# Mixture-of-experts stage: the order of gathers and scatters, identity products at the end, and four idle products on TensorE

## The reference, cut to what matters

```
logits = flat_x @ gate_w.T
scores = softmax(logits).T                     # 16 experts x 2048 tokens
topk_weight, topk_idx = top_k(scores, C)       # C = 256 tokens for each expert
xg = flat_x[topk_idx]                          # gather
g = einsum('ecd,eid->eci', xg, Wg)
u = einsum('ecd,eid->eci', xg, Wu)
h = gelu(g) * u
eo = einsum('eci,edi->ecd', h, Wd) * topk_weight[..., None]
flat_out = zeros.at[topk_idx].add(eo)          # scatter, summed
out = flat_out + shared(x)
x = x + 0.5 * out
```

## Time and profile before

| what | value |
|---|---|
| median of 3 runs | 1263.83 us (1261.38 to 1265.91) |
| the profiled execution's own time | 1263.55 us |
| its span in the trace | 1261.7 us |
| PE busy | 1143.5 us, 91% |
| DVE busy | 865.9 us, 69% |
| ACT busy | 706.6 us, 56% |
| POOL busy | 523.4 us, 41% |

### The profile page before, as it was taken

How to read it: one execution, slowest core, us unless ns; L and a number is a source line. 1 busy time by engine, 2 the same in 40 slices (tenths; PEclk the granted TensorE clock), 3 DMA queues, 4 the chain that set the end, 5 groups by cost and what they waited for, 6 DMA issues and landing times. The chain is left out here.

```text
span 1261.7 us, 19699 instructions
## 1 busy us (share of the span) xinstructions
PE 1143.5 (91%) x6491; PEld 571.9 (45%) x6491; DVE 865.9 (69%) x1903; ACT 706.6 (56%) x887; POOL 523.4 (41%) x548
## 2 busy tenths in 40 slices
PE   4799999999999998869977599999999999778995
PEld 2444444444444484459963122222222223447994
DVE  6466566576666555864436999999999994585442
ACT  3677777777777625212215267767777677421221
POOL 0066666656656600337863013213311321035884
PEclk9899999999999997879998599999999999797998
DMA  4000011001001100516754421232132120322665
GB/s 123 1 7 25 18 26 38 17 24 40 17 24 34 36 18 31 174 29 190 179 107 82 84 64 42 61 51 59 43 64 53 37 51 1 136 70 86 177 160 117
DMA packets 58444, 81.91 MB, mean 65 GB/s; under 512 B 18520, under 2 KB 40412, under 8 KB 57500
## 3 DMA queue, kind: packets, MB, share of 16 engines
q1 hardware_dynamic: 46808, 71.87, 21.4%
q0 software_dynamic: 10944, 8.92, 4.7%
q10 hardware_dynamic: 616, 0.14, 0.1%
HBM read 55.34 MB, written 11.67 MB: 53 GB/s over the span
## 5 line engine op out<-in xcount | busy, mean ns | idle before, releaser
L1771 ACT ACTIVATE at_PR<-psum 128x1024 f32<-128x1024 f32 x256 | 248.0, 1021 | 121.8 <-PE psum L2000 121.6
L1839 DVE TENSOR_REDUCE at_MX<-psum 128x1 f32<-128x512 f32 x468 | 301.0, 685 | 10.5 <-PE psum L1982 6.1
L1708 POOL TENSOR_TENSOR at_PR<-at_PR,at_FAC 128x512 f32<-128x512 f32 x64 | 81.2, 1268 | 293.0 <-ACT at_PR L1771 293.0
L486 ACT ACTIVATE PR<-psum 128x1024 f32<-128x1024 f32 x144 | 140.9, 1026 | 82.2 <-PE psum L770 76.6
L770 PE MATMUL psum<-Q,K 64*128 64x512 f32 (+3 forms) x768 | 143.5, 502 | 1.2 <-ACT PR L486 1.2
L491 ACT ACTIVATE PR<-PR 128x1024 f32<-128x1024 f32 x144 | 144.6, 1062 | 0.0
L782 PE MATMUL psum<-PR,V 128*64 128x512 f32 (+3 forms) x768 | 139.7, 495 | 0.1
L2000 PE MATMUL psum<-at_QS,at_KS 122*128 122x512 bf16 x512 | 136.0, 387 | 2.2 <-DVE at_MX L1835 1.6
L2018 PE MATMUL psum<-at_PR,at_VG 128*32 128x512 f32 x1024 | 136.6, 606 | 0.0
L463 POOL TENSOR_SCALAR_AFFINE_SELECT PR<-PR 128x256 f32<-128x256 f32 (+1 forms) x112 | 57.7, 529 | 167.8 <-ACT PR L491 167.7
L1982 PE MATMUL psum<-at_KM,at_QM 64*128 64x512 bf16 x512 | 104.0, 404 | 18.5 <-DVE at_MX L1835 8.0
(11 more groups left out here) (238 smaller groups left out, 1666.5 us busy)
## 6 DMA issues: line engine op xcount, KB each, us to landing
moe_WE<-in_c_We SPq DMA_DIRECT2D x32, 768.0 KB
XB<-at_r_dram SPq DMA_DIRECT2D x32, 256.0 KB, 3.8
at_QS<-at_SPL SPq DMA_DIRECT2D x72, 64.0 KB
at_KS<-at_SPL SPq DMA_DIRECT2D x72, 64.0 KB
at_KS<-in_c_krows SPq DMA_DIRECT2D x8, 384.0 KB
moe_rows_dram<-XNS SPq DMA_DIRECT2D x2, 1152.0 KB, 10.6
moe_sum_dram<-moe_zeros SPq DMA_DIRECT2D x2, 1024.0 KB, 13.3
moe_spare_dram<-moe_zeros SPq DMA_DIRECT2D x2, 1024.0 KB, 15.6
```

The lines of the kernel that those rows point to most:

```text
L486: act.activation(PR[u][:, :, :], S[(b + u) % 2][:, :, :], ACT.Tanh, scale=SCALE0 / CLAMP).then_inc(z.clamped, 1)
L1708: pool.tensor_tensor(pr, pr, FAC[:, 4 * (s // 2):4 * (s // 2) + 4, :], ALU.mult).then_inc(z.factored, 1)
L1771: act.activation(PR[:, gu % PRS, 2 * r:2 * r + 2, :].rearrange("p h n -> p (h n)"), g.psum[:, 2 * r * BANK:(2 * r + 2) * BANK], ACT.Exp).t ...
L1839: dve.tensor_reduce(MX[:, 4 * (2 * pair + c % 2) + I % 4, khalf:khalf + 1], bank(("max", c))[:, :], AX, ALU.max).then_inc(z.reduced, 1)
```

## The change

It has four parts, in both expert stages.

1. POOL: six gathers first, then scatter 0, then gathers 6 and 7, and from there scatter e and gather e+7 by turns. The waits on the turns of experts 3 to 5 ahead of gathers 5 to 7 are gone.
2. PE does down(e-1) between the two halves of expert e, and DVE writes EO of expert e-1 between the two H of expert e.
3. The end: `merge` is gone. PE multiplies the identity with XB (four products) and then with X (four products). Two quarters of X are reloaded by SP, two by ACT. In the last stage ACT and DVE copy two banks each.
4. Four idle products on TensorE (identity by 512 columns of XT, float32): one after the last product of the search, two after the transposes of the positions, one after `spread(0)`.

```diff
@@ gpsimd
-                for e in range(ahead):
-                    if e >= DEEP:
-                        pool.wait_ge(z.xturned, e - DEEP + 2)
-                    gath(e)
-                pool.wait_ge(z.inited, 16 * lanes)
-                for e in range(E1):
-                    if e + ahead < E1:
-                        pool.wait_ge(z.xturned, e + 1)
-                        pool.wait_ge(z.wcopied, e + 1)
-                        gath(e + ahead)
-                    if e == E1 - 1:
-                        break
...
-                for k in (2, 3):
-                    merge(pool, k, z.merged2)
+                for e in range(first_ahead):
+                    if e == DEEP:
+                        pool.wait_ge(z.xturned, 2)
+                    gath(e)
+                pool.wait_ge(z.inited, 16 * lanes)
+                scatter(0)
+                for e in range(first_ahead, ahead):
+                    gath(e)
+                for e in range(1, E1 - 1):
+                    scatter(e)
+                    if e + ahead - 1 < E1:
+                        wait(pool, z.xturned, e)
+                        wait(pool, z.wcopied, e)
+                        gath(e + ahead - 1)
@@ tensor
+                stir(pe, g, 6, g.XT[:, 0:BANK], 1)
                 pe.wait_ge(z.onehot, 3)
...
                 mm.then_inc(z.posturned, 1)
+                stir(pe, g, 6, g.XT[:, 0:BANK], 2)
                 pe.wait_ge(z.sharedhalf, 4)
...
+                        if e and h == 0:
+                            down(e - 1)
                     if e == 0:
                         spread(QUARTERS - 1)
-                    if e:
-                        down(e - 1)
...
                 spread(0)
+                stir(pe, g, 6, g.XT[:, 0:BANK], 1)
                 list_in(1)
...
                 for k in range(4):
-                    pe.wait_ge(z.merged if k < 2 else z.merged2, k % 2 + 1)
+                    pe.wait_ge(z.rested, k + 1)
+                    pe.matmul(ps[4 + k], g.ident[:, :], g.XB[:, 4 * k:4 * k + 4, :].rearrange("p t d -> p (t d)"),
+                              start=False, stop=False, skip_group_check=True)
+                for k in range(4):
+                    pe.wait_ge(z.spared[k], 16)
                     pe.matmul(ps[4 + k], g.ident[:, :], g.X[:, 4 * k:4 * k + 4, :].rearrange("p t d -> p (t d)"),
                               start=False, stop=True, skip_group_check=True).then_inc(z.resummed, 1)
@@ vector
...
+                        if e and h == 0:
+                            rows_out(e - 1)
...
-                for k in range(2):
-                    merge(dve, k, z.merged)
+                if final is not None:
+                    for k in (1, 3):
+                        dve.wait_ge(z.resummed, k + 1)
+                        dve.tensor_copy(g.XN[:, 4 * k:4 * k + 4, :].rearrange("p t d -> p (t d)"), ps[4 + k]).then_inc(z.copied2, 1)
@@ scalar
+                act.wait_ge(z.scattered[0], landed(E1 - 2))
+                for k in (1, 3):
+                    reload(act, k)
```

More of the change, by code:

```diff
@@ L949, in stage_experts @@
         "gelued hidden down scaled compared").split())
-    lanes, onehot_from = 2, 3
-    ahead = DEEP * lanes
+    lanes, onehot_from, ahead, first_ahead = 2, 3, 8, 6
     z.weights = [sem(f"{n}_weights{b}") for b in range(DEEP)]
@@ L958, in stage_experts @@
     z.scattered = [sem(f"{n}_scattered{v}") for v in range(lanes)]
-    z.masked, z.rested, z.merged, z.merged2, z.copied, z.written = (
-        sem(n + "_" + x) for x in "masked rested merged merged2 copied written".split())
+    z.masked, z.rested, z.copied, z.copied2, z.written = (sem(n + "_" + x) for x in "masked rested copied copied2 written".split())
     z.resummed, z.table, z.kept = (sem(n + "_" + x) for x in "resummed table kept".split())
@@ L1004, in stage_experts, with reload @@
         c = g.i
[L1005 to L1009, removed]
+        def reload(eng, k):
+            eng.dma_start(g.X[:, 4 * k:4 * k + 4, :], sums[0].rearrange("(p t) d -> p t d", p=P)[:, 4 * k:4 * k + 4, :]
+                          ).then_inc(z.spared[k], 16)
         spreads = [ps[f % 2][:, BANK // 2:BANK // 2 + 2 * PART] for f in range(QUARTERS)]
@@ L1034, in _ @@
                 sp.wait_ge(z.scattered[0], landed(E1 - 2))
-                for k in range(4):
-                    sp.dma_start(g.X[:, 4 * k:4 * k + 4, :], sums[0].rearrange("(p t) d -> p t d", p=P)[:, 4 * k:4 * k + 4, :]
-                                 ).then_inc(z.spared[k], 16)
+                for k in (0, 2):
+                    reload(sp, k)
                 if final is not None:
                     for k in range(4):
-                        sp.wait_ge(z.copied, k + 1)
+                        sp.wait_ge(z.copied2 if k % 2 else z.copied, k // 2 + 1)
                         sp.dma_start(final.rearrange("b s d -> (b s) d").rearrange("(t p) d -> p t d", p=P)[:, 4 * k:4 * k + 4, :],
@@ L1059, in _, with scatter @@
                 pool.wait_ge(z.stored, 16)
[L1060 to L1071 removed]
+                def scatter(e):
                     pool.wait_ge(z.scaled, 2 * e + 2)
@@ L1113, in _ @@
                     expert(e)
+                if final is None:
+                    act.activation(MX[:, 0:1], g.eps[:, 0:1], ACT.Sqrt).then_inc(z.table, 1)
+                act.wait_ge(z.scattered[0], landed(E1 - 2))
+                for k in (1, 3):
+                    reload(act, k)
                 if final is not None:
-                    for k in range(4):
+                    for k in (0, 2):
                         act.wait_ge(z.resummed, k + 1)
@@ L1236, in expert, with rows_out @@
                 def expert(e):
[L1237 to L1252, removed]
+                    dve.wait_ge(z.gathered[e % ahead], 32 * (e // ahead) + 32)
+                    wait(dve, z.scaled, 2 * (e - DEEP + 1))
+                    dve.tensor_scalar(WT[:, e % DEEP, :], XG[:, e % ahead, :, D + e:D + e + 1].rearrange("p k o -> p (k o)"), 0.5, None,
+                                      ALU.mult).then_inc(z.wcopied, 1)
+                    for h in range(2):
+                        dve.wait_ge(z.gelued, 2 * e + h + 1)
+                        wait(dve, z.down, e - 1)
+                        dve.tensor_tensor(H[:, e % 2, 2 * h:2 * h + 2, :].rearrange("p k c -> p (k c)"), GL[:, h, :],
+                                          ps[6 + h][:, :], ALU.mult).then_inc(z.hidden, 1)
+                        if e == 0 and h == 0:
+                            index(QUARTERS - 1)
+                        if e and h == 0:
+                            rows_out(e - 1)
+                def rows_out(d):
                     dve.wait_ge(z.down, d + 1)
@@ L1268, in mask @@
                                       IDXF[:, k:k + 1], None, ALU.is_equal).then_inc(z.masked, 1)
-                for e in range(E1 + 1):
+                for e in range(E1):
                     expert(e)
```

4 lines of the change are left out of this document (2 added, 2 removed).

## The result

| | median us | lowest to highest | runs |
|---|---|---|---|
| before | 1265.54 | 1261.38 to 1268.09 | 16 |
| changed | 1257.41 | 1252.68 to 1261.69 | 16 |

The medians differ by 8.1 us, where 9.1 were forecast (1254.8 for 1263.85). The recorded ratio, which is not the quotient of the two medians, is 0.9941 with a 95% interval of 0.9929 to 0.9953, so faster by 7.5 us, between 5.9 and 9.0. 1257.41 lies within the range of 1250 to 1260. The profiled execution took 1257.14 us, its span is 1255.4 for 1261.7.

What follows compares the result with a forecast made beforehand. It took PE, busy 91% of the span, and POOL as a second bound whose late last scatter holds both stage ends. 1263.55 less 3.9 (middle stage) and 5.0 (last stage) gave 1254.65, stated as 1254.8, range 1250 to 1260.

Steps and rivals of the forecast that it cites:

- What bounds the end: Both stage ends: PE waits for the last scatter, late because POOL is a second bound, and X's reload; middle hole 7.66 us.
- Part 1 and 2, POOL: POOL queue in both stages: new order and earlier EO bring the last scatter 4.0 us earlier in each, without new stalls.
- Scatter 0 starts at about 567.1: POOL, middle stage: EO of expert 0 ready at 566.9, scatter 0 after a 1.5 us wait, where it stood at 578.93.
- Part 2 on PE: PE per expert: early down costs nothing inside the loop, but one-hot products start 1.65 us later per stage.
- The rival of a pause in each expert: PE ahead of down(e-1): thirty experts pay b, 1259.3 at b = 0.15; small pauses chance 0.10, large ones, slower 0.04.
- cover of 0.3 to 0.4 us: PE ahead of down(e-1): about 1.9 us needed for the second H, 3.6 us of turn and both halves available.
- Part 3: Middle stage's end: identity products on XB, then X, without a pause, done at 662.7; stage gains 3.7 to 4.1, taken as 3.9.
- PE finds them there: Middle stage's end: X issued 4.0 us earlier at 653.8, last quarters there by 658.8, before PE finishes XB at 659.2.
- Last stage: End of the kernel: identity products end at 1253.0, last copy at 1253.8 where it ended at 1258.85; 5.0 us gained.
- Part 4: Idle products before the first expert: clock falls again before 555, first half keeps 3.7 us; gain taken as 0.
- the 1.9 us of the rival: First expert of each stage: idle products hold the clock, expert 0 ends 1.9 us earlier, total 1251.0; chance 0.12.
- The sum: Whole kernel: 1263.55 - 3.9 - 5.0 = 1254.65, stated as 1254.8 since the median of runs is 0.3 higher.

Runs made afterwards that it cites:

- pool_old: Changed kernel with POOL's old order of gathers and scatters restored, the other parts kept: median 1261.93 us, ratio 0.9979.
- pool_only: Kernel before with only POOL's new order of gathers and scatters added: median 1261.07 us, ratio 0.9967.
- end_only: Kernel before with only the new end added (identity products for XB and X, reloads on two queues, split copies): median 1260.94 us, ratio 0.9967.
- seven: Changed kernel with seven gathers ahead of scatter 0 in place of six: median 1256.85 us, ratio 0.9935.
- seven_last: Changed kernel with seven gathers ahead of scatter 0 and, in expert 15 only, down(14) and its EO behind both halves again: median 1251.60 us, ratio 0.9901.
- after_again: The changed kernel run and profiled once more without any edit: median 1257.56 us, ratio 0.9949.
- one_queue: Changed kernel with all four quarters of X reloaded by SP, none by ACT: median 1256.16 us, ratio 0.9933.
- seven_last_bare: Changed kernel with seven gathers ahead of scatter 0, the old order in expert 15 and no idle products: median 1254.88 us, ratio 0.9920.
- keep_clock: Changed kernel with three more idle-product calls per expert stage, after list_in(1), turn(0) and spread(2): median 1260.61 us, ratio 0.9948.
- last_order: Changed kernel with down(14) and EO of expert 14 behind both halves of expert 15 again, all others early: median 1253.92 us, ratio 0.9913.
- down_late: Changed kernel without part 2, down(e-1) and EO of e-1 behind both halves again: median 1257.08 us, ratio 0.9958.
- no_idle: Changed kernel without its four idle products between search and first expert: median 1256.96 us, ratio 0.9930.

## Why the prediction was right

**What bounds the end.** Right. pool_old, pool_only and end_only show it from three sides: the end waits for the later of two things, PE's own products and X's reload behind the last scatter. The change had to shorten both. By the medians what one part gives alone is less than half of the sum; the ratios leave that open.

**Part 1 and 2, POOL.** Mechanism right, size off by a quarter: the last scatter was to come 4.0 us earlier in each stage and came 2.97 and 2.69. The failed term is "Scatter 0 starts at about 567.1", 11.84 after the first gate product; it was 12.77. EO was ready at 569.28 (568.67 + 0.61), 11.97 after it, where 11.64 was forecast, and POOL began 0.8 us later, where I had allowed 0.2. So the wait of some 1.5 us ahead of scatter 0 was 2.49; behind it POOL has no gap above 0.35, as forecast. I had the hole in the working and took it as small; seven shows that a gather fits into it at no cost.

**Part 2 on PE.** Forecast 1.65 later for the one-hot products, measured 2.13 and 1.99 in stage time. The price of the last down was right: from the end of EO of expert 0 to the first one-hot product seven takes 81.56 us in both stages, and seven_last, whose only difference is the order in the last expert, 79.90 in both, so 1.66. What the sum lacked is ahead of that. The early down should have brought EO of expert 0 1.75 us sooner after the first gate product; it brought 1.42 and 1.36 (11.97 for 13.39, 12.54 for 13.90). And there is a small pause: one down, some 26 us after the first gate product, waits 0.15 us in the middle stage and 0.18 in the last:

```profile
581.03 1.89 PE L1402 MATMUL psum<-moe_XGT,moe_WE 128*128 128x256 f32 x8
583.07 1.16 PE L1420 MATMUL psum<-moe_WE,moe_H 128*128 128x128 f32 x8 [0.15 <-DVE moe_H L1246]
```

ACT's step for that H started at 581.70, about 0.7 us late: PE's next row stands at 580.81, and other such steps start 0.2 after theirs (577.49 for 577.29). The pause is no property of the early down: it stands in the five kernels with late steps of ACT (0.15 to 0.71 us, in pool_old up to 1.61) and in none of after_again, one_queue, seven, seven_last and seven_last_bare. In the kernel before ACT is late at the same place, and nothing showed, since down had more cover there. Why ACT is late stays open. The rival of a pause in each expert did not occur: the other downs start without a wait, so the cover of 0.3 to 0.4 us holds.

**Part 3.** "PE finds them there" holds by the thinnest margin. X was issued 2.5 us earlier in stage time, not 4.0: a later scatter (1.0) and 0.48 us more for it to land (6.33 from the last scatter's start to the issue, 5.85 before). That PE came later as well, by 0.5, is why it still met X in time. Two terms were off in the same sense, and the gain was set by PE: 3.97 for 3.9. That this is so close is in part luck. DVE's first statistics row came 3.31 us earlier in stage time where 3.7 were forecast (108.67 before, 105.36 after), and what follows gained 0.66 where up to 0.4 were allowed.

**Last stage.** 4.67 for 5.0, the difference being the later one-hot start. In the repeat it gained 6.16, so the size is known to about 1.5 us.

**Part 4.** Right: 3.75 us for the first eight rows, clock 0.50 before the first expert. Where I was incomplete is what the products do: they hold the clock up through most of the list part. Whether a clock held up to the end of it would be worth the 1.9 us of the rival stays open: in keep_clock the first eight rows took 1.97 us, and a late release of 2.5 us hid what that was worth. The Trainium skill's page "TensorE: Matmul & The Clock Gate", section "Why this matters for your kernels", asks for no long PE-idle gap between bursts; the trace does not bear that out as sufficient, since the list products from 552.0 to 562.0 leave no gap above 0.82 us and the clock fell among them, at 555.2.

**The sum.** 8.64 in the stages for 8.9 forecast. The median moved by 8.1. (1254.65 and the 0.28 that the median lay above the profiled run give 1254.93, not 1254.8; nothing hangs on it.)

## What to carry to other kernels

An in-order queue that is nearly as loaded as the bound engine turns each microsecond that it wastes at a stage's start into one at its end: look for the first piece of its final work that stands, ready, behind something else. When two chains meet at an end, price an edit to one of them only up to where the other takes over, and read from the timeline which wait each half-measure leaves: alone they gave 2.8 and 2.9 us by the medians here, all parts together 8.1, though the intervals are too wide to show that the whole is more than the sum. After such a change look for the next pair: here one more gather ahead and the old order in a single expert gave another 3.3 to 4.7 us by the stages, although the one without the other could not be told from nothing (seven) or barely (last_order).

## What the runs showed of the hardware

- In the changed kernel the granted clock fell to 0.50 at 555.2. From 552.0 on PE had been busy for about half of the time, with small products and no gap above 0.82 us. In keep_clock, with more wide products among them, it stayed at 1.00 until 562.0 in one stage and fell at 1142.2 in the other.
- An indirect DMA on POOL that waits for DVE began 0.8 us after DVE's row ended when POOL stood idle (569.28 and 570.08 in the changed kernel, 0.79 or 0.80 at scatter 0 in both stages of pool_only and down_late as well). A gather DMA comes every 1.25 us, a scatter DMA every 1.86.
- In keep_clock DVE, ACT and POOL were released at 562.82, 562.86 and 563.10, one after another within 0.3 us, DVE 2.8 us and ACT 2.5 us after the products they waited for had ended (559.98 and 560.35). The profile calls the releaser remote. Such late releases, above 0.6 us, stand in the profiles of before, the changed kernel, pool_old, no_idle, keep_clock and last_order and in none of the other eight, the changed kernel's second profile among them. What they are stays open.
